# Latent attention: the mixing of a unit moved two steps earlier behind its scores, with two buffers of turned tiles in place of four

## The reference, cut to what matters

```python
h = layernorm(x) * ln_scale + ln_bias
c_q, c_kv = h @ w_down_q.T, h @ w_down_kv.T            # 64 wide each
q, k, v = up-projections of c_q, c_kv, c_kv             # 16 heads of 64, all 2048 tokens
q, k = rope(q), rope(k)
attn = softmax((q @ k.T) / 8)
out = (attn @ v) merged over heads @ w_out.T + x
```

## Time and profile before

| | |
|---|---|
| median of 3 runs | 1986.32 us (1982.45 to 1987.06) |
| the profiled execution's own time | 1989.45 us |
| its span, first to last instruction | 1987.4 us |
| PE busy | 1843.7 us, 93% |
| DVE busy | 1583.3 us, 80% |
| ACT busy | 1389.9 us, 70% |
| POOL busy | 1028.9 us, 52% |
| mean granted TensorE clock | 0.964 of full speed |
| latent loop | about 617 to 1856 us of the span |

### The profile page before, as it was taken

How to read it: one execution, slowest core, us unless ns; L and a number is a source line. 1 busy time by engine, 2 the same in 40 slices (tenths; PEclk the granted TensorE clock), 3 DMA queues, 4 the chain that set the end, 5 groups by cost and what they waited for, 6 DMA issues and landing times. The chain is left out here.

```text
span 1987.4 us, 35423 instructions
## 1 busy us (share of the span) xinstructions
PE 1843.7 (93%) x11066; PEld 897.7 (45%) x11066; DVE 1583.3 (80%) x2378; ACT 1389.9 (70%) x2776; POOL 1028.9 (52%) x1027
## 2 busy tenths in 40 slices
PE   5777898989868999999999999999999999999798
PEld 3553586558643343433434333334343343433446
DVE  5788865686656889888888888888988888888455
ACT  5555784478535888787788887788877878888321
POOL 0646742574216646646655654764664665565200
PEclk9898898989888999999999999999999999999799
DMA  1100302021043676776767766767676676776353
GB/s 39 67 1 6 82 4 75 6 56 29 15 181 86 173 176 167 180 171 156 183 159 181 176 160 172 174 170 176 169 178 168 161 176 164 183 172 161 93 122 72
DMA packets 176645, 250.52 MB, mean 126 GB/s; under 512 B 20256, under 2 KB 167456, under 8 KB 175296
## 3 DMA queue, kind: packets, MB, share of 16 engines
q1 hardware_dynamic: 176448, 248.11, 49.8%
HBM read 28.75 MB, written 2.36 MB: 16 GB/s over the span
## 5 line engine op out<-in xcount | busy, mean ns | idle before, releaser
L1664 DVE TENSOR_REDUCE g.lowest<-g_score 128x1 f32<-128x1024 f32 x514 | 605.5, 1219 | 155.5 <-PE g_score L1634 155.5
L1678 ACT ACTIVATE g.probs<-g_score,g.lowest 128x1024 f32<-128x1024 f32 x514 | 567.8, 1109 | 204.7 <-DVE g.lowest L1664 202.9
L1634 PE MATMUL g_score<-g.keys,g.queries 64*128 64x512 f32 x2056 | 506.1, 611 | 15.2 <-PEq L1470 8.3
L1774 DVE STREAM_TRANSPOSE g.blocks<-g.probs 128x768 f32<-128x768 f32 x512 | 467.0, 950 | 0.9
L1694 PE MATMUL g_mix_ps<-g.far,mid.y_tok 128*64 128x512 f32 x1560 | 377.4, 605 | 0.0
L1634 PEld LDWEIGHTS g_score<-g.keys,g.queries 64*128 64x128 f32 x2056 | 181.3, 188 | 284.0 <-ACT g.probs L1678 165.7
L1734 POOL TENSOR_TENSOR g.scaled<-g.scaled,g.coef 128x1024 f32<-128x1024 f32 x66 | 125.1, 1896 | 248.7 <-ACT g.scaled L1726 248.7
L1654 PEld LDWEIGHTS g_turned<-top.ident,g.probs 128*128 128x128 f32 x1024 | 107.6, 141 | 195.4 <-issue 193.8
L1654 PE MATMUL g_turned<-top.ident,g.probs 128*128 128x128 f32 x1024 | 168.5, 287 | 0.0
L1423 POOL TENSOR_TENSOR g.queries<-mid.y_tok,g.exchanged 64x512 f32<-64x512 f32 x128 | 162.2, 1267 | 9.8
L1694 PEld LDWEIGHTS g_mix_ps<-g.far,mid.y_tok 128*64 128x64 f32 x1560 | 94.9, 136 | 145.0 <-issue 144.2
(11 more groups left out here) (373 smaller groups left out, 2848.2 us busy)
## 6 DMA issues: line engine op xcount, KB each, us to landing
g.far<-g.blocks SPq DMA_DIRECT2D x1028, 192.0 KB, 3.7
e.share<-shares SPq DMA_DIRECT2D x8, 1024.0 KB, 17.4
g.far<-g.near SPq DMA_DIRECT2D x7, 768.0 KB, 12.3
lt.early<-turns SPq DMA_DIRECT2D x2, 2048.0 KB, 10.2
lt.early<-la0.v SPq DMA_DIRECT2D x6, 512.0 KB, 9.4
lt.early<-la1.v SPq DMA_DIRECT2D x6, 512.0 KB, 9.9
top.upto<-stored_mixers SPq DMA_DIRECT2D x33, 64.0 KB, 2.8
g.waves<-g_waves SPq DMA_DIRECT2D x1, 2048.0 KB, 8.0
```

The lines of the kernel that those rows point to most:

```text
L1634: nc.tensor.matmul(score[:, 2 * pair + odd], queries[rows, turn, head, cols], keys[rows, turn, head, pair * CH:(pair + 1) * CH], start=Tru ...
L1664: nc.vector.tensor_reduce(lowest[:, unit, half, r:r + 1], score[:, 2 * half:2 * half + 2].rearrange("p b n -> p (b n)"), AX.X, ALU.max, ne ...
L1678: nc.scalar.activation(probs[:, r % 2, half * 2 * CH:(half + 1) * 2 * CH], score[:, 2 * half:2 * half + 2].rearrange("p b n -> p (b n)"), ...
L1774: ins = nc.vector.transpose(blocks[:, r, :, REST * half:REST * (half + 1)].rearrange("p j t c -> p t j c"), probs[:, r % 2, at:at + REST * ...
```

## The change

The mixing of unit V now has its near quarter in step 1 of unit V+1, its far quarters in steps 2 and 3 of V+1 and in step 0 of V+2. In steps 0 and 4 the output product stands ahead of the mixing. The wait for landed blocks moves from step 0 to step 2. ScalarE copies the mixed values in steps 1 and 5, ahead of the copy of the output, and no longer in steps 3 and 7; `exchange` 1 moves from step 0 to the step 7 before it. `blocks` has two buffers, used in turn, and `turn_blocks` waits for the sends of two steps before. SyncE sends each unit's four blocks within the unit. Ahead of the loop six pairs of a mixing of zeros are done in place of two, behind it two far pairs in place of six.

```diff
--- before.py
+++ after.py
@@ -1367,7 +1367,7 @@
     with Space(nc, "g") as sp:
         c = sp.sb("c", [P, S])
         waves = sp.sb("waves", [P, HALVES, 2, QH])
-        blocks = sp.sb("blocks", [P, RT, 4, FAR, 32])
+        blocks = sp.sb("blocks", [P, 2, 4, FAR, 32])
         mixers = blocks[:, 0:2].rearrange("p r j t c -> p (r j t c)")[:, 0:(2 + HEADS_G) * D].rearrange("p (h n) -> p h n", n=D)
         stored_mixers = nc.dram_tensor("stored_mixers", (2 + HEADS_G, P, D), F32).ap()
         keys = sp.sb("keys", [P, 2, 2, S // 2])
@@ -1453,9 +1453,8 @@
             zeros = near[:].rearrange("p a t n -> p (a t n)")[:, 0:4 * RUN]
             for r in range(RT):
                 sync.dma_start(far[:, 0, 4 * r:4 * r + 4], zeros).then_inc(m["far_zeroed"], 16)
-            for r in range(RT - 1):
+            for r in range(RT):
                 sync.dma_start(far[:, 1, 4 * r:4 * r + 4], zeros).then_inc(sent[r], 16)
-            sync.dma_start(blocks[:, RT - 1], zeros).then_inc(sent[RT - 1], 16)
 
         def set_front(pool):
             nc.gpsimd.memset(near[:], 0.0).then_inc(m["zeroed"], 1)
@@ -1655,7 +1654,7 @@
             ins.then_inc(m["turn_done"], 1)
 
         def copy_tiles(act, w, r):
-            nc.scalar.activation(near[:, w, :, r * P:(r + 1) * P], turned[:].rearrange("p (t n) -> p t n", n=P), ACT.Copy)\
+            nc.scalar.activation(near[:, w, :, r * P:(r + 1) * P], turned[:, 0:NEAR * P].rearrange("p (t n) -> p t n", n=P), ACT.Copy)\
                 .then_inc(m["near_copied"], 1)
 
         def row_max(dve, unit, r, half, G):
@@ -1768,16 +1767,16 @@
         def turn_blocks(dve, r, G):
 
             dve.wait_ge(m["exp_done"], 2 * G + 2)
-            dve.wait_ge(sent[r], 16 * (G - r) + PRIMED)
+            dve.wait_ge(sent[(r + 2) % RT], 16 * (G - r) + PRIMED + 64 * (r // 2))
             for half in range(2):
                 at = half * 2 * CH + TURN * P
-                ins = nc.vector.transpose(blocks[:, r, :, REST * half:REST * (half + 1)].rearrange("p j t c -> p t j c"),
+                ins = nc.vector.transpose(blocks[:, r % 2, :, REST * half:REST * (half + 1)].rearrange("p j t c -> p t j c"),
                                           probs[:, r % 2, at:at + REST * P].rearrange("p (t j a) -> p t j a", j=4, a=32))
             ins.then_inc(m["blocks_turned"], 1)
 
         def send_blocks(sync, w, r):
             for i in range(4):
-                sync.dma_start(far[:, w, 4 * r + i], blocks[32 * i:32 * i + 32, r]).then_inc(sent[r], 16)
+                sync.dma_start(far[:, w, 4 * r + i], blocks[32 * i:32 * i + 32, r % 2]).then_inc(sent[r], 16)
 
         def exchange(act, n, k):
             act.wait_ge(m["piece_taken"], n + 1)
@@ -1807,7 +1806,7 @@
                     pool.wait_ge(m["order"], 10 * n + 8 + 2 * crossed)
                 pool.sem_inc(m["parts_ready"], 1)
 
-        MIXED_AT = (range(2, 4), range(4, 6), range(6, 8), range(0, 2))
+        MIXED_AT = (range(6, 8), range(0, 2), range(2, 4), range(4, 6))
 
         with nc.Block() as block:
 
@@ -1820,21 +1819,17 @@
                             for w in range(2):
                                 U = 8 * g + 2 * j + w
                                 G, H = 4 * U, 8 * g + 2 * j
-                                sync.wait_ge(m["blocks_turned"], G + 2)
-                                send_blocks(sync, 1 - w, 3)
                                 sync.wait_ge(m["out_full"], H + 1 + w)
                                 load_mixer(sync, 1 - w, 2 * (2 * i + turn + (j + 3) // NC) + w)
+                                sync.wait_ge(m["blocks_turned"], G + 3)
                                 sync.wait_ge(m["mix_done"], U + 1)
                                 send_blocks(sync, w, 0)
                                 if j == 0 and w == 0:
                                     sync.wait_ge(m["piece_full"], 4 * g + 1)
                                     load_w(sync, turn, g + 2)
-                                sync.wait_ge(m["blocks_turned"], G + 4)
-                                send_blocks(sync, w, 1)
-                                sync.wait_ge(m["blocks_turned"], G + 5)
-                                send_blocks(sync, w, 2)
-                sync.wait_ge(m["blocks_turned"], 4 * UNITS + 2)
-                send_blocks(sync, 1, 3)
+                                for r in range(1, RT):
+                                    sync.wait_ge(m["blocks_turned"], G + r + 3)
+                                    send_blocks(sync, w, r)
                 for r in range(RT):
                     sync.wait_ge(sent[r], 64 * UNITS + PRIMED)
                 for w in range(2):
@@ -1877,7 +1872,7 @@
             def _(pe):
                 for k in range(2):
                     score_pair(pe, k, 0, 0, 0, 0)
-                mix(pe, 0, range(0, 2))
+                mix(pe, 0, range(0, 6))
                 pieces(pe, 1, 0)
                 pe.sem_inc(m["out_full"], 1)
                 with pe.Fori(0, PAIRS_G // 2) as i:
@@ -1901,13 +1896,6 @@
                                         score_pair(pe, half, on, head, chunk, at)
                                     pe.wait_ge(m["near_copied"], G + 1)
                                     turn_tiles(pe, r)
-                                    if r == 0:
-                                        for k in range(RT):
-                                            pe.wait_ge(sent[k], 64 * U + PRIMED - 64)
-                                    if r == 3:
-                                        pe.wait_ge(m["mixed_ready"], U + 2)
-                                        pe.wait_ge(m["near_copied"], 4 * U + 1)
-                                    mix(pe, w if r < 3 else 1 - w, MIXED_AT[r])
                                     if step == 0:
                                         pe.wait_ge(m["out_taken"], H + 1)
                                         pe.wait_ge(m["piece_taken"], 4 * g + j + 1)
@@ -1919,7 +1907,16 @@
                                         pe.wait_ge(m["mixed_ready"], U + 1)
                                         pe.wait_ge(mixer_loaded[1], 16 * (4 * g + j + 1))
                                         output(pe, mixer_now[1])
-                                    elif step == 5:
+                                    if r == 1:
+                                        pe.wait_ge(m["mixed_ready"], U + 2)
+                                        pe.wait_ge(m["near_copied"], 4 * U + 1)
+                                        mix(pe, 1 - w, range(0, 2))
+                                    else:
+                                        if r == 2:
+                                            for k in range(RT):
+                                                pe.wait_ge(sent[k], 64 * U + PRIMED)
+                                        mix(pe, w if r == 0 else 1 - w, MIXED_AT[r])
+                                    if step == 5:
                                         pe.wait_ge(m["out_taken"], H + 3)
                                         if j < NC - 1:
                                             pe.wait_ge(w_loaded[1 - turn], 16 * (i + 1 + turn))
@@ -1934,7 +1931,7 @@
                 output(pe, mixer_now[0])
                 for k in range(RT):
                     pe.wait_ge(sent[k], 64 * (UNITS - 1) + PRIMED)
-                mix(pe, 0, range(2, 8))
+                mix(pe, 0, range(6, 8))
                 pe.wait_ge(m["mixed_ready"], UNITS + 2)
                 pe.wait_ge(m["out_taken"], UNITS + 2)
                 output(pe, mixer_now[1])
@@ -1996,7 +1993,8 @@
                 for half in range(2):
                     exps(act, 0, 0, half, 0, free=False)
                 take_pieces(act, 0)
-                exchange(act, 0, 0)
+                for k in range(2):
+                    exchange(act, 0, k)
                 with act.Fori(0, PAIRS_G // 2) as i:
                     for turn in range(2):
                         g = 2 * i + turn
@@ -2009,23 +2007,22 @@
                                     unit = (2 * j + w + (r + 1) // RT) % 4
                                     step = 4 * w + r
                                     if step == 0:
-                                        for k in range(1, 3):
-                                            exchange(act, 4 * g + j, k)
+                                        exchange(act, 4 * g + j, 2)
                                     elif step == 1:
+                                        take_mixed(act, U + 1)
                                         take_output(act, H)
                                     elif step == 2:
                                         falls(act, H - 1)
                                         exchange(act, 4 * g + j, 3)
-                                    elif step == 3:
+                                    elif step == 5:
                                         take_mixed(act, U + 1)
-                                    elif step == 5:
                                         take_output(act, H + 1)
```

(4 more changed lines are left out.)

## The result

The changed kernel takes 2005.07 us in the median of 5 runs (2000.87 to 2009.17), the kernel before 1986.32 (1982.45 to 1987.49): a ratio of 1.010, interval 1.0084 to 1.0115, slower by 0.84 to 1.15%. The forecast was 2005.6. The profiled execution took 2005.07 us with a span of 2003.1.

What follows compares the result with a forecast made beforehand. The prediction took TensorE's own sequence of matmuls to bound the kernel. Order +12.2, exchange +7.6, outer loop's turns -0.5 and the rest 0 made +19 us, from 1986.3 to 2005.6 us; range 1992 to 2022.

Steps and rivals of the forecast that it cites:

- What bounds the kernel: Latent loop: TensorE goes from one matmul to the next, its own sequences summing to 37.6 us for a pair of units.
- Part 1, the order: Steps 0 and 4: output ahead of mix costs TensorE +0.19 us an output, +12.2 us with 64 outputs.
- X: Time from turn to output on TensorE in the new order of steps 0 and 4, taken as 0.58 us.
- Y: Time from output to mix on TensorE in the new order of steps 0 and 4, read as 1.09 us.
- rival by which all weight loads are pulled ahead: TensorE: weights are loaded ahead at every switch, so the kernel is not slower; chance 0.08.
- Part 2, the exchange: ScalarE, step 7: two exchanges release the next scores late, +0.27 us a pair in 28 pairs, +7.6 us.
- Part 3, the sends: Blocks and DMA queue: VectorE's waits for landed sends with two buffers cost 0, upper end 25 us.
- rival of too few buffers: VectorE waits for landings at turns of steps 2, 3, 6 and 7: +25 to +64 us above forecast; chance 0.10.
- Part 4, the ends: Four more pairs of zero mixing ahead of the loop, +3.5 us; four fewer in the tail, -3.5 us; net 0.
- The outer loop's turns: What moves out of step 0 gives back at most 0.5 us at each of three turns; counted as -0.5.
- the faster rival: The outer loop's three turns, 4.0 us or less each, vanish, with order and exchange free: 1976 us; chance 0.02.
- the forecast alone: Time range from the order's 8 to 17 us plus the exchange's 0 to 13 us: 1998 to 2016 us.

Runs made afterwards that it cites:

- exchange_moved: The kernel before with the second exchange moved from step 0 to the step 7 before it, where the copy of mixed values still stands; 2007.1 us, ratio 1.0110.
- order_back: The changed kernel with the mixing ahead of the output again in steps 0 and 4; 1992.5 us, ratio 1.0039 to the kernel before.
- exchange_back: The changed kernel with the second exchange in step 0 again; 1996.0 us, ratio 1.0062 to the kernel before.
- both_back: The changed kernel with the mixing ahead of the output and the second exchange in step 0 again; 1986.0 us, ratio 1.0011 to the kernel before.
- output_first: The kernel before with the output ahead of the mixing in steps 0 and 4; 2000.1 us, ratio 1.0079.
- four_buffers: As both_back, but with four buffers of blocks and the wait on sends four steps old; 1982.3 us, ratio 0.9997 to the kernel before.
- no_zero_mix: As both_back, but with two pairs of zero mixing ahead of the loop in place of six; 1975.9 us, ratio 0.9963 to the kernel before.

## Why the prediction was right

The time was forecast within a microsecond, which owes something to luck: the runs of one kernel lie up to 12 us apart, and the median of the kernel before moves by 2 us from one occasion to the next. The mechanism owes nothing to it, since both costs were found by themselves. By its steps:

- **What bounds the kernel.** TensorE's own sequence, read from starts. Confirmed: every edit of the sequence came out in the pair to 0.02 us (exchange_moved, whose lateness was taken too large, to 0.13), and all else (two buffers, spread sends, earlier waits, other copies) left it at 37.62.
- **Part 1, the order.** X = 0.58 and Y = 1.09 were taken from rows elsewhere in the trace and both found (0.59, 1.09). +0.19 an output was forecast, 0.20 measured by three comparisons (order_back with the changed kernel, exchange_back with both_back, output_first with the kernel before). With 64 outputs 12.8 us; the sum had 12.2. From start to start the 0.20 us is 0.10 between output and mix (1.09, where output to scores had 0.99) and 0.10 between scores and turn (1.92, where scores that follow an output had 1.82). The rival by which all weight loads are pulled ahead is out: the mixing's load starts only when the output's are done. Whether such a load meets the conditions that the prediction quotes for that rival, no row here tells. That a change of tile shape drains the array is the rule of the Trainium skill's TensorEngine Tiling (Array Packing), section Key Properties. All these timelines agree with its sign: output to scores 0.88 us from load to load, output to mix 1.09. That it is a drain that takes the time is not shown; no run separates a drain from a weight load that comes late.
- **Part 2, the exchange.** +0.27 us a pair forecast and measured, 7.6 us; the larger dose of exchange_moved follows the same sum. The moved copies in steps 1 and 5 cost nothing, as forecast.
- **Part 3, the sends.** No wait in steady pairs; 1.1 us to spare where 0.8 was forecast. The rival of too few buffers is out for the steady pairs. It leaves three waits behind the outer loop's turns, of which one cost TensorE 1.11 us where the prediction counted nothing.
- **Part 4, the ends.** +3.36 and -3.44 us for +3.5 and -3.5.
- **The outer loop's turns.** 0.5 us was counted in all. In the profiled executions what the three turns add fell from 10.5 to 6.6 us. Of these 3.9 us, 0.8 is the exchange not costing anything there, as the prediction had it; so 3.1 us stand where it had 0.5. But the medians don't bear this out: both_back and four_buffers have the pair of the kernel before and a head and a tail that cancel, and 4.2 and 5.1 us less at the turns in their profiles, yet their ratios are 1.0011 and 0.9997. So it is not shown that the change makes the turns cheaper, and the faster rival, which had them gone, is out.
- **The range.** The prediction gives "the forecast alone" as 1998 to 2016, from 8 to 17 us for the order and 0 to 13 for the exchange. By these bounds the low end is 1986.3 + 8 = 1994; 1998 is the order at its forecast with the exchange at nothing. The outer range, 1992 to 2022, holds either way.

The measured terms add up: 31 distances of 0.67 us make 20.8, the first pair has 0.2 more, the turns 3.9 less, the ends 0.1 less, which is 17.0; the stages around the loop, which the change doesn't touch, differ by -1.3 between the two executions; together 15.7 us, the difference of the spans. The medians differ by 18.8: the profiled execution of the kernel before was 3.1 us above its median, that of the changed kernel was its median. Without the 3.9 us at the turns the terms give 20.9. So what one pair of profiles shows at the turns is not to be taken as the mean.

## What to carry to other kernels

On an engine without gaps look at what stands next to what: moving a block of 64-row matmuls from between 128-row and 64-row ones to between two 128-row ones cost 0.2 us each time, with not one matmul more. Work moved on an engine with slack has to fit the slack of the very step it goes to: the same two exchanges were free in the step that was 1 us longer and cost 0.27 us in the one that wasn't. Such costs can be summed ahead from starts of like neighbours anywhere in the trace. Steady pairs can be free of a wait that still comes behind a turn of the outer loop. And filler ahead of a loop counts like any other work of the engine that sets the pace: with both costs undone and two or four pairs of zero mixing in place of six, the kernel was faster than both the one before and the changed one.

## What the runs showed of the hardware that was not expected

A turn of the outer loop adds 0.9 to 4.1 us in these profiles. In the kernel before more than half of it (6.5 of 10.5 us) is an idle TensorE that waits for nothing the profile names; in no_zero_mix this idle time is 0.3 to 0.8 us a turn. Leaving out two or four pairs of zero mixing ahead of the loop took the turns from 2.1 us each (both_back) to 1.1 to 1.4; adding four pairs to the kernel before left them at 3.2, from 3.5. Each of these figures but no_zero_mix's comes from one execution. What decides them stays open.
